# Time mixing begun in eight of the iterations 2 to 12 instead of iterations 5 to 12, its results kept in DRAM, and every helper step, plain product and low part placed by kind of iteration

## The chip, the cores and the metric

One core of a Trainium2 chip runs the whole program. The metric is the device time of one launch in microseconds (us). The kernel before took 924.7 us, the median of 3 runs (924.21 to 929.85). The profiled execution is one further run: 924.3 us, of which its trace spans 922.5 us.

## The reference

The input x is 8 sequences of 512 tokens with 128 channels, all fp32. Four residual layers follow each other, each on a layer norm of x:

```python
x = x + attention(norm(x))          # one head, causal, 128 channels
x = x + ffn(norm(x))                # 32 experts of width 64, top 4, capacity, and a shared expert
x = x + attn_b(norm(x))             # RWKV: time mixing, then channel mixing
x = x + ffn(norm(x))                # the same ffn and weights again
```

Inside attn_b, time mixing is a layer norm (ln1), three mixes of a token with the one before it, three 128x128 products for k, v and r, a recurrence over the 512 tokens with running maximum (wkv), a gate sigmoid(r), and an output product. Its result `u2 = u + time mixing` then goes into channel mixing: a layer norm (ln2), mixes, a 128x512 product, relu and square, a 512x128 product and a gate. The expert ffn is computed densely: `silu(x w1) * (x w3) * routing weight`, times w2, for all 32 experts in pairs.

## The kernel before

**Iterations and slots.** The ffn is the backbone. It runs for 8 sequences in layer 0 and for 8 in layer 1, so there are 16 iterations g = 0 to 15. An iteration has 17 units: 16 pairs of experts (`PAIRS`) and the shared expert. Each of the engines' programs walks `slot` from 0 to 16 (17 on VectorE, ScalarE and GpSimd), does unit `slot`, and between the units does steps of the other layers, each at a slot that is written out by hand. Nothing plans this at run time. Each engine works through its own list in order, so a step that waits holds up all units behind it on that engine.

**A unit.** TensorE multiplies the 512 tokens by w1 and w3 into PSUM banks `pa` and `pb`, two of each (L742 to L744). Operands are split into a high and a low part, so one product is three matmuls. ScalarE applies silu, or tanh in the slots of `TANH_UNITS` (L526, L528). VectorE multiplies with `pb` into `m_v` (L1043; with tanh L1049 and L1055). GpSimd multiplies with the routing weight `m_wb` into `m_h` (L418). Then the down product. On a split unit ScalarE copies the high part `m_hh` (L667), VectorE or GpSimd subtracts it to get the low part `m_hl` (L309), and TensorE does three matmuls (L760 to L762). On a native unit TensorE takes `m_h` itself in one plain fp32 product (L754, two records in the trace). `NATIVE` and `NATIVE_UNITS` say which: units 1, 3, ..., 15 of iterations 5 to 12, none elsewhere. `LOW_ON_POOL` says which low parts GpSimd makes.

TensorE may write the pair of banks of unit p only when VectorE has done `m_v` of unit p - 2, and VectorE may write `m_v` of unit p only when GpSimd has done `m_h` of unit p - 2.

**What shares the iterations.** `att` is attention of a sequence, `pro` is norm and router of the next iteration's sequence, `tmix` is time mixing and `cmix` is channel mixing:

| iteration | steps beside the ffn |
|---|---|
| 0 to 4 | att (sequence g + 2), pro |
| 5 | att, pro, tmix 0 |
| 6 to 12 | pro, tmix g - 5, cmix g - 6 |
| 13 | pro, cmix 7 |
| 14 | pro |
| 15 | none |

`cmix` begins with the output product of time mixing (TensorE L907) and the sum into `t_u2` (VectorE L1277), and it reads `t_u2` in SBUF until slot 10.

**VectorE in time mixing.** In slots 0 to 9: row statistics, the three mixes (L1213), the maximum scan (L1218) and the exponents (L1223 to L1228). In slots 11 to 17: two scans (L1233, L1235), products and sums (L1239 to L1247), four reciprocals (L1304), and the last two products (L1259, L1264).

**Queues.** SyncE issues all DMAs but two. `spread_weights(q)` waits for the router's result `r_wT` (ScalarE L581), writes it to DRAM (L345), waits for that, and reads it back with broadcast in four groups of four units, two 512 KB transfers each (L365), into a ring of two groups. Group 2 waits until GpSimd has done unit 3 of the iteration. Outputs are stored from the same queue (L371).

Of the kernel before, what the change touches and what calls it, by code (L numbers as in the profile page):

```python
# [9 lines left out]

# [47 lines left out]
N_MATS = 12  # L58


def hybrid_kernel(nc, x_in, att_mats, mats, key_in, vecs, w_gate, w1_in, w3_in, w2_in, x_out):
    with ExitStack() as ctx:  # L62
# [9 lines left out]
        def wide(ap):  # L72
# [114 lines left out]

        w_scratch = nc.dram_tensor("w_scratch", [2 * B, GROUPS, GP, 2, S], F32, kind="Internal").ap()
# [8 lines left out]
            "m_hl_dve m_hl_pool m_y m_ys m_yT m_x in_w2f "  # L197
# [47 lines left out]
        def native(g, p):  # L245

            return g in NATIVE and p in NATIVE_UNITS

# [17 lines left out]
        def front(step):  # L266

            step(att=1, pro=0, lead=5)
# [9 lines left out]
        def low_on_pool(g, p):  # L278

            return p in LOW_ON_POOL[sum(g >= first for first in POOL_FROM) - 1]  # L280

# [34 lines left out]
        def out_bank(tmix, cmix):  # L316

            return pq if tmix is None and cmix is None else pv
# [7 lines left out]
        def _(sp):  # L326
# [14 lines left out]

            def spread_weights(q):
# [4 lines left out]
                for j in range(GROUPS):  # L347
# [37 lines left out]
        def _(pool):  # L385
# [42 lines left out]
            def pro_step(q, slot):  # L428
                if slot == 2:
                    rsqrt(r_rs[:, :], r_ve[:, :], "r_vedone", q + 1, "r_rstd")  # L430
                if slot == 6:
# [5 lines left out]
            def time_step(m, slot):  # L437
                if slot == 0:
                    rsqrt(t_rs[:, :], t_ve[:, :], "t_ve", 2 * m + 2, "t_rstd")
                if slot == 4:  # L440
# [3 lines left out]
                if slot == 8:  # L444
# [4 lines left out]
                if slot == 9:  # L449
# [5 lines left out]
            def channel_step(m, slot):  # L455
                if slot == 10:
                    pool.wait_ge(sig["t_u2"], m + 1)
                    pool.wait_ge(sig["t_u"], m + 1)
# [4 lines left out]
                if slot == 6:  # L463
# [3 lines left out]
            def iteration(g=None, att=None, tmix=None, cmix=None, pro=None, lead=0):  # L467
                for slot in range(-lead, UNITS + 1):
# [5 lines left out]
                    if att is not None and slot == 0:  # L474
                        rsqrt(a_rs[:, :], a_ve[:, :], "a_vedone", att + 1, "a_rstd")
                    if cmix is not None:
# [905 lines left out]
```

## Time and profile before

| | |
|---|---|
| median of 3 runs | 924.7 us |
| profiled execution, span of its trace | 924.3 us, 922.5 us |
| start until unit 0 of iteration 0 | 62.4 us |
| TensorE (PE) busy | 818.3 us, 89% |
| VectorE (DVE) busy | 741.4 us, 80% |
| GpSimd (POOL) busy | 633.9 us, 69% |
| ScalarE (ACT) busy | 537.9 us, 58% |
| DMA, mean busy share of 16 engines by slice | 0 to 9 tenths, mostly 3 or 4 |

The busy time of TensorE is modelled: consecutive matmuls overlap in it, so what a matmul costs is read from the start of one to the start of the next. The boundary of an iteration is here the start of its first matmul into `pa`. Those starts lie at 62.4, 110.5, 159.4, 208.3, 260.0, 308.9, 371.9, 431.1, 489.9, 548.8, 607.6, 666.4, 725.3, 784.2, 835.4 and 875.7 us.

### The profile page before, as it was taken

Reading aid. Unit: us, or ns where it says so; the run is one execution under the profiler, and the core shown is the slowest. Engines: PE = TensorE matmul, PEld = TensorE weight load, DVE = VectorE, ACT = ScalarE, POOL = GpSimd, SP = SyncE. Lnnn points to the kernel's source line nnn. Section 1 sums busy time; section 2 is a strip of 40 time slices with the busy share of each in tenths; the row PEclk is TensorE's granted clock in tenths of the full one; section 3 lists DMA queues with packets and bytes.
Section 4 is the critical chain, followed back from the end, with each engine's and each line's share of the span. In section 5 each row is a group of like instructions: output and inputs, shape, how many; then the busy total and the mean of one; then the engine's idle time right before and its main releaser. Section 6 shows DMA issues by size and latency. Waiting matters only on the chain. (4 is left out here: it accounts for less than half of the span.)

```text
span 922.5 us, 12867 instructions
## 1 busy us (share of the span) xinstructions
PE 818.3 (89%) x3874; PEld 627.0 (68%) x3874; DVE 741.4 (80%) x1593; ACT 537.9 (58%) x1002; POOL 633.9 (69%) x467
## 2 busy tenths in 40 slices
PE   4579999998999986988979899898898998999997
PEld 2357777777777764766757667586675766778785
DVE  3557767686777779899898998998989989787764
ACT  2246566664656664673855747557476574575654
POOL 5417777777687865685767858678587686576675
PEclk9599999999999999999999999899999999999999
DMA  9033333425243430614305242143332441425262
GB/s 305 0 95 77 82 78 82 102 53 131 49 96 91 95 92 3 137 47 94 74 21 128 56 89 55 43 108 90 66 75 57 95 103 43 99 60 135 74 141 66
DMA packets 46500, 78.12 MB, mean 85 GB/s; under 512 B 3168, under 2 KB 12512, under 8 KB 46048
## 3 DMA queue, kind: packets, MB, share of 16 engines
q1 hardware_dynamic: 46144, 77.10, 35.6%
q8 instruction: 32, 0.52, 0.3%
q10 hardware_dynamic: 288, 0.20, 0.1%
q14 instruction: 36, 0.29, 0.1%
HBM read 74.14 MB, written 3.15 MB: 84 GB/s over the span
## 5 line engine op out<-in xcount | busy, mean ns | idle before, releaser
L418 POOL TENSOR_TENSOR m_h<-m_v,m_wb 128x512 f32<-128x512 f32 x256 | 366.2, 1436 | 207.3 <-DVE m_v L1043 106.5
L526 ACT ACTIVATE m_th<-pa 128x512 f32<-128x512 f32 x232 | 138.3, 596 | 198.9 <-PE pa L744 168.2
L309 DVE TENSOR_TENSOR m_hl<-m_h,m_hh 128x512 fp32r<-128x512 f32 x130 | 111.4, 858 | 81.3 <-ACT m_hh L667 81.2
L742 PE MATMUL pa<-m_xh,w1h 128*128 128x512 f32 x272 | 143.3, 527 | 31.4 <-DVE m_v L1055 31.0
L1043 DVE TENSOR_TENSOR m_v<-m_th,pb 128x512 f32<-128x512 f32 x216 | 145.9, 676 | 16.4 <-ACT m_th L526 9.4
L667 ACT ACTIVATE m_hh<-m_h 128x512 fp32r<-128x512 f32 x208 | 130.6, 628 | 35.8 <-POOL m_h L418 34.8
L742 PE MATMUL pb<-m_xh,w3h 128*128 128x512 f32 x272 | 110.2, 405 | 10.1 <-DVE m_v L1043 9.8
L309 POOL TENSOR_TENSOR m_hl<-m_h,m_hh 128x512 fp32r<-128x512 f32 x78 | 108.0, 1384 | 7.1 <-ACT m_hh L667 7.1
L744 PE MATMUL pb<-m_xh,w3l 128*128 128x512 f32 x272 | 108.6, 399 | 0.0
L744 PE MATMUL pa<-m_xh,w1l 128*128 128x512 f32 x272 | 108.3, 398 | 0.0
L743 PE MATMUL pa<-m_xl,w1h 128*128 128x512 f32 x272 | 108.1, 397 | 0.0
L743 PE MATMUL pb<-m_xl,w3h 128*128 128x512 f32 x272 | 108.1, 397 | 0.0
L742 PEld LDWEIGHTS pa<-m_xh,w1h 128*128 128x128 f32 x272 | 52.3, 192 | 58.2 <-DVE m_v L1055 40.7
L760 PE MATMUL py<-m_hh,w2h 128*128 128x512 f32 x208 | 83.2, 400 | 2.6 <-POOL m_hl L309 2.6
L762 PE MATMUL py<-m_hl,w2h 128*128 128x512 f32 x208 | 82.9, 399 | 0.0
L761 PE MATMUL py<-m_hh,w2l 128*128 128x512 f32 x208 | 82.6, 397 | 0.0
L742 PEld LDWEIGHTS pb<-m_xh,w3h 128*128 128x128 f32 x272 | 51.7, 190 | 28.1 <-DVE m_v L1043 16.1
L754 PE MATMUL py<-m_h,w2f 128*128 128x512 f32 x128 | 65.2, 591 | 0.0
L743 PEld LDWEIGHTS pa<-m_xl,w1h 128*128 128x128 f32 x272 | 52.5, 193 | 17.7 <-issue 13.9
L744 PEld LDWEIGHTS pb<-m_xh,w3l 128*128 128x128 f32 x272 | 52.2, 192 | 12.1
L744 PEld LDWEIGHTS pa<-m_xh,w1l 128*128 128x128 f32 x272 | 51.9, 191 | 12.0
L743 PEld LDWEIGHTS pb<-m_xl,w3h 128*128 128x128 f32 x272 | 52.0, 191 | 11.5
(211 smaller groups left out, 1651.2 us busy)
## 6 DMA issues: line engine op xcount, KB each, us to landing
m_wb<-w_scratch SPq DMA_DIRECT2D x126, 512.0 KB, 6.5
x_sb<-in_x SPq DMA_DIRECT2D x8, 256.0 KB, 7.2
m_wb<-in_w SPq DMA_DIRECT2D x2, 1024.0 KB, 6.9
x_out<-x_sb SPq DMA_DIRECT2D x8, 256.0 KB, 6.9
f_kk<-in_w SPq DMA_DIRECT2D x1, 1024.0 KB, 9.9
w_scratch<-r_wT SPq DMA_DIRECT2D x16, 64.0 KB, 1.6
m_wb<-w_scratch SPq DMA_DIRECT2D x8, 128.0 KB, 3.0
mt<-in_mats SPq DMA_DIRECT2D x1, 768.0 KB, 8.1
```

What stands on the lines that cost most here:

```text
L309: eng.tensor_tensor(m_hl[:, at, :], hidden(g, p), m_hh[:, at, :].bitcast(F32), ALU.subtract)\
L418: pool.tensor_tensor(hidden(g, p), gated(g, p), m_wb[:, p % (GRING * GP), :], ALU.mult).then_inc(sig["m_h"], 1)
L526: ins = act.activation(m_th[:, p % 2, :], pa[p % 2][:, :], ACT.Silu)
L667: act.activation(m_hh[:, halves_at(g, p), :], hidden(g, p), ACT.Copy).then_inc(sig["m_hh"], 1)
L742: pe.matmul(ps[:, :], high[:, p, :], xh, start=True, stop=False)
L743: pe.matmul(ps[:, :], high[:, p, :], xl, start=False, stop=False)
L744: return pe.matmul(ps[:, :], low[:, p, :], xh, start=False, stop=True)
L754: pe.matmul(py[:, :], w2f[:, NATIVE_UNITS.index(p), :], hidden(g, p), start=False, stop=False)\
L760: pe.matmul(py[:, :], w2h[:, p, :], hh, start=(p == 0), stop=False)
L761: pe.matmul(py[:, :], w2l[:, p, :], hh, start=False, stop=False)
L762: pe.matmul(py[:, :], w2h[:, p, :], hl, start=False, stop=(p == UNITS - 1)).then_inc(sig["m_y"], 1)
L1043: dve.tensor_tensor(gated(g, p), m_th[:, r, :], pb[r][:, :], ALU.mult).then_inc(sig["m_v"], 1)
```

## The change

The results of the time mixing of sequences 0 to 5 (`KEPT`) are written to a DRAM tensor `u_scratch` and read back into `t_u2` in the iteration of their channel mixing. Time mixing is cut into `begin` (up to the exponentials and the r product), `finish` (from the two scans to the gate) and `out` (output product and sum). `begin` is done in iterations 2, 3, 4, 5, 6, 8, 10, 12, `finish` in 2, 3, 4, 5, 7, 9, 11, 12, and `out` in the iteration after `finish`. Attention and channel mixing stay in their iterations. Each iteration has one of seven modes, and each step's slot is a tuple over modes:

| iteration | mode | beside ffn and pro |
|---|---|---|
| 0, 1 | 0 | att |
| 2 to 5 | 1 | att, begin, finish, and out from 3 on |
| 6, 8, 10 | 3 | cmix, begin, out |
| 7, 9, 11 | 4 | cmix, finish |
| 12 | 2 | cmix, begin, finish, out |
| 13 | 5 | cmix, out |
| 14, 15 | 6 | none |

```diff
-NATIVE = range(B - 3, 2 * B - 3)
 NATIVE_UNITS = (1, 3, 5, 7, 9, 11, 13, 15)
-LOW_ON_POOL = ((0, 4, 6, 7, 8, 9, 11, 12, 14, 15), (0, 4, 8, 12), (6, 14), (6, 9, 12, 15), (2, 9, 14))
-POOL_FROM = (0, B - 3, B - 2, 2 * B - 3, 2 * B - 2)
+MODES = (0, 0, 1, 1, 1, 1, 3, 4, 3, 4, 3, 4, 2, 5, 6, 6)
+NATIVE = ((9,), (1, 3, 5, 7, 9, 11, 13, 15), (1, 3, 5, 7, 9, 11, 13, 15), (1, 3, 5, 7, 9, 13, 15), (1, 3, 5, 7, 9, 11, 13, 15), (1,), (9, 13))
+LOW_ON_POOL = ((4, 6, 7, 8, 11, 12, 14, 15), (4, 6, 8, 12, 14), (6, 10, 14), (6, 11, 14), (0, 6, 8, 12, 14), (0, 6, 9, 12, 15), (2, 4, 8, 14))
+KEPT = 6
+BEGIN_AT = {2: 0, 3: 1, 4: 2, 5: 3, 6: 4, 8: 5, 10: 6, 12: 7}
+BEGINS = {1: 0, 2: 1, 3: 2}
+FINISHES = {1: 0, 2: 1, 4: 2}
+OUTS = {1: 0, 2: 1, 3: 2, 5: 3}
...
+def plan(g):
+    finishes = {2: 0, 3: 1, 4: 2, 5: 3, 7: 4, 9: 5, 11: 6, 12: 7}
+    outs = {3: 0, 4: 1, 5: 2, 6: 3, 8: 4, 10: 5, 12: 6, 13: 7}
+    return Plan(g, g + 2 if g < LATE else None, BEGIN_AT.get(g), finishes.get(g), outs.get(g),
+                g - LATE if LATE <= g < LATE + B else None, g + 1 if g < 2 * B - 1 else None, MODES[g])
...
+        def kept(eng, m):
+            if m < KEPT:
+                eng.wait_ge(sig["u_in"], 16 * m + 16)
+            else:
+                eng.wait_ge(sig["t_u2"], m + 1)
...
+            def keep(it):
+                if it.cmix is not None and it.cmix < KEPT:
+                    sp.wait_ge(sig["u_out"], 16 * it.cmix + 16)
+                    if it.cmix > 0:
+                        sp.wait_ge(sig["f_x"], 2 * it.cmix)
+                    sp.dma_start(wide(t_u2[:, :, :]), u_scratch[it.cmix]).then_inc(sig["u_in"], 16)
+                if it.out is not None and it.out < KEPT:
+                    sp.wait_ge(sig["t_u2"], it.out + 1)
+                    sp.dma_start(u_scratch[it.out], wide(t_u[:, :, :])).then_inc(sig["u_out"], 16)
...
                         sp.wait_ge(sig["m_h"], done(PAIRS * (q - 1) + GP * (GROUPS - GRING + j + 1)))
+                    if j == GRING:
+                        keep(plan(q))
```

Some of the slots on VectorE, TensorE and ScalarE (tuples of two are over modes 0 and 1; tuples of three are over the modes of `BEGINS` or `FINISHES` in the order of their values; tuples of four are over modes 2 to 5):

```diff
             # VectorE
-                if slot == 1:
+                if slot == (2, 0)[mode]:            # attention: normalise a_xn
-                if slot == 9:
+                if slot == (9, 8, 9)[mode]:         # begin: maximum scan, exponents
-                if slot == 11:
+                if slot == (13, 13, 12)[mode]:      # finish: two scans, two products
-                if slot == 12:
+                if slot == (13, 14, 12)[mode]:      # finish: two sums
-                if slot == 14:
+                if slot == (13, 16, 13)[mode]:      # finish: reciprocal 0
-                if slot == 15:
+                if slot == (16, 17, 15)[mode]:      # finish: reciprocal 1
-                if slot == 14:
+                if slot == (15, 16, 14)[mode]:      # finish: reciprocals 2, 3
-                if slot == 3:
-                    dve.wait_ge(sig["t_u2"], m + 1)
+                if slot == (3, 5, 5, 2)[mode]:      # channel mixing: row statistics of t_u2
+                    kept(dve, m)
...
             # TensorE
-                if slot == 3:
+                if slot == (4, 2)[mode]:            # attention: transposes of a_xn
-                if slot == 10:
+                if slot == (10, 9, 12, 12)[mode]:   # channel mixing: first key product
...
             # ScalarE
-                if slot == 14:
+                if slot == (14, 13, 14, 15, 15, 17, 14)[mode]:   # router: r_wT
```

(The comments are this document's, the rest is the diff.) The instructions themselves are the same ones, except for the 12 transfers of 256 KB and the exchange of split for plain products.

## Rows read from the trace of the kernel before

**Rows 1.** Busy time by iteration: 2 (first row), 4, 5, 9, 10, 13

```profile
core 0: us, PE busy (x) PEld busy (x) DVE busy (x) ACT busy (x) POOL busy (x), PEclk, DMA share, GB/s
...
159.40:208.30 48.90, 46.61 (x239) 37.45 (x238) 36.09 (x90) 30.59 (x59) 37.53 (x30) 1.00 0.38 87
...
260.00:308.90 48.90, 46.60 (x240) 37.44 (x239) 35.92 (x90) 30.59 (x59) 37.57 (x30) 1.00 0.39 88
308.90:371.90 63.00, 53.31 (x244) 38.90 (x243) 53.08 (x115) 34.09 (x66) 41.72 (x32) 0.97 0.31 70
...
548.80:607.60 58.80, 54.29 (x249) 40.76 (x249) 54.14 (x107) 36.31 (x66) 42.07 (x29) 0.94 0.32 74
607.60:666.40 58.80, 52.03 (x249) 38.58 (x248) 54.14 (x107) 36.48 (x66) 42.09 (x29) 1.00 0.34 77
...
784.20:835.40 51.20, 48.16 (x245) 37.93 (x245) 38.58 (x82) 32.39 (x59) 32.30 (x24) 1.00 0.38 88
```

**Rows 2.** The same: early in iteration 5; iterations 9 and 13 cut at unit 11

```profile
311.00:330.00 19.00, 18.62 (x90) 14.20 (x88) 15.83 (x47) 13.08 (x29) 17.45 (x14) 1.00 0.55 122
...
548.80:579.40 30.60, 30.50 (x138) 22.61 (x137) 26.31 (x61) 21.81 (x44) 22.57 (x16) 1.00 0.43 98
579.40:607.60 28.20, 23.79 (x114) 18.15 (x113) 27.82 (x47) 14.50 (x23) 19.50 (x13) 0.88 0.20 47
784.20:813.50 29.30, 27.61 (x130) 21.48 (x130) 22.54 (x47) 18.45 (x35) 18.74 (x14) 1.00 0.42 90
813.50:835.40 21.90, 20.55 (x116) 16.45 (x115) 16.04 (x36) 13.93 (x24) 13.55 (x11) 1.00 0.34 85
```

**Rows 3.** Timeline of TensorE, iteration 9: start, duration, instruction, idle time before it

```profile
577.52 0.39 PE L760 MATMUL py<-m_hh,w2h 128*128 128x512 f32 x1
...
578.21 0.39 PE L942 MATMUL pv<-f_xh,key_h 128*128 128x512 f32 x1
...
581.14 1.02 PE L754 MATMUL py<-m_h,w2f 128*128 128x512 f32 x2
582.00 1.05 PE L921 MATMUL pu<-mt,a_pT 128*128 128x128 f32 x8
...
586.88 0.79 PE L742 MATMUL pa<-m_xh,w1h 128*128 128x512 f32 x1 [3.12 <-DVE m_v L1055]
```

**Rows 4.** Timeline of VectorE, iteration 9, the end of time mixing

```profile
590.52 1.21 DVE L1233 TENSOR_TENSOR_SCAN t_aa<-t_ea,t_xk 128x512 f32<-128x512 f32 x1
...
594.99 0.68 DVE L309 TENSOR_TENSOR m_hl<-m_h,m_hh 128x512 fp32r<-128x512 f32 x1
...
596.19 0.68 DVE L1244 TENSOR_TENSOR t_xr<-t_xr,t_eb 128x512 f32<-128x512 f32 x1
596.79 1.79 DVE L1247 TENSOR_TENSOR t_n<-t_n,t_xv 128x512 f32<-128x512 f32 x1
...
600.92 2.57 DVE L1304 RECIPROCAL t_ri<-t_xr 128x128 f32<-128x128 f32 x3
...
603.95 0.94 DVE L1304 RECIPROCAL t_ri<-t_xr 128x128 f32<-128x128 f32 x1
...
605.35 0.68 DVE L1259 TENSOR_TENSOR t_ri<-t_n,t_ri 128x512 f32<-128x512 f32 x1
606.07 1.65 DVE L1264 SCALAR_TENSOR_TENSOR t_n<-t_r,t_ri 128x512 f32<-128x512 f32 x1
```

**Rows 5.** Waits in iterations 0 to 4: total us, times, longest

```profile
PE pu L720 <- DVE a_xn L1019: 10.4, 5, 2.9
...
DVE a_xn L1019 <- POOL a_rs L403: 7.9, 5, 2.7
```

**Rows 6.** Timeline of iteration 9: GpSimd at unit 3, then VectorE at unit 5

```profile
559.92 1.29 POOL L418 TENSOR_TENSOR m_h<-m_v,m_wb 128x512 f32<-128x512 f32 x1 [0.19 <-DVE m_v L1043]
...
564.08 0.68 DVE L1043 TENSOR_TENSOR m_v<-m_th,pb 128x512 f32<-128x512 f32 x1
```

**Rows 7.** The output stores of 256 KB (L371), from issue to landing

```profile
DMA to landing us min/median/max: 2.3/6.9/7.2
```

More of the change, by code:

```diff
@@ L9 @@
 from contextlib import ExitStack
+from typing import NamedTuple
 import concourse.bass as bass
@@ L58, with begun @@
 N_MATS = 12
+class Plan(NamedTuple):
+    g: int | None = None
+    att: int | None = None
+    begin: int | None = None
+    finish: int | None = None
+    out: int | None = None
+    cmix: int | None = None
+    pro: int | None = None
+    mode: int = 0
+def begun(g):
+    return sum(1 for at in BEGIN_AT if at < g)
+def plan(g):
[3 more added lines that the diff above has]
+                g - LATE if LATE <= g < LATE + B else None, g + 1 if g < 2 * B - 1 else None, MODES[g])
 def hybrid_kernel(nc, x_in, att_mats, mats, key_in, vecs, w_gate, w1_in, w3_in, w2_in, x_out):
@@ L266, in front @@
         def front(step):
-            step(att=1, pro=0, lead=5)
+            step(Plan(att=1, pro=0), lead=5)
         def is_late(g):
@@ L278, in low_on_pool @@
         def low_on_pool(g, p):
-            return p in LOW_ON_POOL[sum(g >= first for first in POOL_FROM) - 1]
+            return p in LOW_ON_POOL[MODES[g]]
         pool_lows = [k for k in split_units if low_on_pool(*divmod(k, UNITS))]
@@ L674, in out_copy, with iteration @@
                 act.activation(m_y[:, :], py[:, :], ACT.Copy).then_inc(sig["m_ys"], 1)
-            def iteration(g=None, att=None, tmix=None, cmix=None, pro=None, late=False, lead=0):
+            def iteration(it, lead=0):
+                g = it.g
                 for slot in range(-lead, UNITS + 1):
                     if g is not None and slot < UNITS:
-                        unit(g, slot, late)
+                        unit(g, slot, is_late(g))
                         split_high(*unit_before(g, slot, SPLIT_LAG))
-                    if slot == 3:
+                    if slot == (2, 2, 3, 3, 3, 3, 3)[it.mode]:
@@ L695, in _ @@
-            for g in range(1, B - 3):
-                iteration(g, att=g + 2, pro=g + 1)
-            iteration(B - 3, att=B - 1, tmix=0, pro=B - 2)
-            iteration(B - 2, tmix=1, cmix=0, pro=B - 1, late=True)
-            iteration(B - 1, tmix=2, cmix=1, pro=B, late=True)
-            iteration(B, tmix=3, cmix=2, pro=B + 1, late=True)
-            for g in range(B + 1, 2 * B - 3):
-                iteration(g, tmix=g - (B - 3), cmix=g - (B - 2), pro=g + 1, late=True)
-            iteration(2 * B - 3, cmix=B - 1, pro=2 * B - 2, late=True)
@@ L704, in _ @@
-            iteration(2 * B - 2, pro=2 * B - 1, late=True)
-            iteration(2 * B - 1, late=True)
+                    if it.att is not None:
+                        att_step(it.att, slot, it.mode)
+                    if it.cmix is not None:
+                        channel_step(it.cmix, slot, it.mode - 2)
+                    if it.pro is not None:
+                        pro_step(it.pro, slot + lead, it.cmix, it.mode)
+                    if it.begin is not None:
+                        time_begin(it.begin, slot, it.pro, BEGINS[it.mode])
@@ L706, in _ @@
+            iteration(Plan(att=0))
+            front(iteration)
+            for g in range(2 * B):
+                iteration(plan(g))
             for p in range(UNITS - SPLIT_LAG, UNITS):
@@ L889, in time_step @@
                     turn(pq, t_hn, "t_tr")
-                if slot == 8:
+                if slot == (9, 8, 8)[mode]:
                     pe.wait_ge(sig["t_xk"], 3 * m + 3)
```

363 lines of the change are left out of this document (170 added, 193 removed).

## The prediction

> **What bounds the kernel now.** I read the busy time of the engines by iteration first, since the change moves work between iterations and removes none. An iteration with attention alone takes 48.9 us with VectorE busy 36; one with time and channel mixing takes 58.8 us with VectorE busy 54.1; iteration 5, with attention and time mixing, takes 63.0 us with VectorE busy 53.1; iteration 13, with channel mixing alone, takes 51.2 us with VectorE busy 38.6 [rows 1]. So there are light and heavy iterations for VectorE, and TensorE has 47 to 54 us in all of them.
>
> Cutting iterations 9 and 13 at unit 11 shows which engine sets the pace where. In the first 30.6 us of iteration 9 TensorE is busy 30.5 and VectorE idles 4.3. In the remaining 28.2 us VectorE is busy 27.8 and TensorE 23.8. The same last six units of iteration 13, which have no time mixing, take 21.9 us [rows 2]. So a heavy iteration is bound by TensorE in its first eleven units and by VectorE in its last six. The timeline shows how: TensorE stands 3.1 us before unit 12 until VectorE has given up a bank [rows 3]. What fills VectorE there is the second half of time mixing: 590.52 to 594.99 (4.5 us), 596.19 to about 598.5 (2.3), 2.6 and 0.9 of reciprocals, and 2.4 from 605.35 to its end, together 12.7 us [rows 4]. The change takes this half out of iterations 6, 8 and 10 and the other half out of 7, 9 and 11; the price is that iterations 2, 3 and 4 become heavy.
>
> **Iterations 2 to 5.** They take 212.5 us now (159.4 to 371.9). Each becomes like iteration 5. VectorE then has 53.1 us [rows 1], less one low part (0.7, as at 594.99), plus, in 3 to 5, the sum into `t_u` (0.7 as well, an operation of that size) and the last two products of the time mixing before, 2.4 [rows 4], which for iteration 5 now fall after its end. That makes 52.4 for iteration 2 and 55.5 for each of 3, 4 and 5. To this comes what VectorE idles. Iteration 5 idles 9.9 now, iteration 9 idles 4.7 [rows 1]. The least that rows support is 3.2 in the early stretch of iteration 5 plus 0.4 in the late stretch of iteration 9, 3.6 [rows 2]. Iteration 5 is the only one of its kind now and shares its slots with iterations 0 to 4 and 6 to 12; with slots of its own, and the low parts spread otherwise, I take 4.1, between that least and the 4.7 of iteration 9. The sum is 56.5 + 3 x 59.6 = 235.3, so +22.8 us. The ends: 3.6 gives +20.8, and 9.9 gives +46.
>
> TensorE's addition there, three plain products and eight native units a piece, is covered: a native unit costs 0.86 us (581.14 to 582.00) against 0.69 for a split one (577.52 to 578.21) [rows 3], so eight cost 1.4 us, under a VectorE that has 55. If VectorE were no longer the bound, these 1.4 us would appear four times.
>
> **Iterations 6 to 11.** They take 353.4 us now (371.9 to 725.3). In 6, 8 and 10 the second half of time mixing is gone. Their first eleven units stay at 30.6, as TensorE's work there is the same; their last six fall to the 21.9 of iteration 13, since VectorE has 27.8 - 12.7 = 15.1 us left there. Two native units in that stretch add 0.3. That is 52.8, and I take 53.0. In 7, 9 and 11 the first half is gone and the second stays. First part: 29.3 as in iteration 13, plus five native units (0.9), minus the output product of time mixing (about 0.4, an estimate: half of the 0.9 that four times as many columns of plain fp32 take in one native product), 29.8. Last part: VectorE's 16.0 of iteration 13 plus 12.7, minus three low parts that are now native or on GpSimd (2.1), minus the last two products, which fall into the next iteration's part bound by TensorE (2.4): 24.2, which is over TensorE's 21.9 and so counts. That is 54.0. Together 3 x 53.0 + 3 x 54.0 = 321.0, so -32.4 us. The ends: -20 if the burst of 12.7 us in four or five slots is not absorbed by two banks and TensorE pays another 2 us in each of the six, and -40 if the last parts of all six come down to 21.9.
>
> **The reload.** `t_u2` is read back in iterations 6 to 11. SyncE issues it after GpSimd's unit 3, which ends at 561.2 in iteration 9; VectorE comes to the statistics after its unit 5, at 564.8 [rows 6]. That leaves 3.6 us. No transfer out of this scratch is in the trace. A 256 KB transfer took 2.3 us at the least and 6.9 in the median, where others lie ahead of it [rows 7]. At that point the ring's transfers of group 1, issued at the iteration's start, are through, and those of group 2 are issued behind the reload. So I take 2.3 and a cost of nothing, hidden by units 4 and 5; the other end is 0.2 + 6.9 - 3.6 = 3.5 us per iteration, 21 us. The six stores stand in the same queue in front of group 2, which GpSimd wants four units later, over 8 us; they cost nothing unless the queue is late by more than that. SyncE's own waits before both are for things done an iteration, or two slots, earlier; behind them only group 2 and 3 and the next router's write are queued.
>
> **The small rest.** In iterations 0 to 4 VectorE waits up to 2.7 us for GpSimd's `a_rs`, which stands behind unit 0, and TensorE then stands 2.9 us for the normalised attention input [rows 5]. In iterations 0 and 1 both steps come one slot later, which I count as 0.5 each, -1.0 us. It could be nothing, or 2 each. In iterations 2 to 5 the step moves to slot 0, which makes VectorE wait there for GpSimd; that lies in the idle time I counted. Iterations 12 to 15 and the start keep their work but for a low part here and a native unit there, and slots: -0.5, between -3 and +3, as nothing in the trace prices a slot by itself.
>
> **Sum.** -1.0 + 22.8 - 32.4 + 0 - 0.5 = -11.1 us against the profiled execution's 924.3, that is 913.2. The median of the runs shown is 0.4 higher than that execution, which is less than I can claim to know: I put it at 913.
>
> **A rule on the clock.** The granted clock of TensorE is 0.88 in the last part of iteration 9, where it waits for VectorE, and 1.00 in that of iteration 13 [rows 2]. Yet iteration 9 with a mean of 0.94 and iteration 10 with 1.00 both take 58.8 us [rows 1]: the lower of the two levels, 1.2 instead of 2.4 GHz, falls into time that VectorE sets. So the sum has no term for it. The Trainium skill ("TensorE: Matmul & The Clock Gate", "Part 1: The HAM clock gate") says that an idle array is put to 1.2 GHz and is given 2.4 GHz again once busy, and warns of kernels whose waits bring this on again and again; by that rule the change would pay in iterations 2 to 4 and be paid in 6 to 11. As a mechanism of this kernel it is the fourth rival below.
>
> **The rivals.** About 1% (9 us) is what a measurement of this kernel can tell from no change.
> - *Iterations 2 to 5 pack no better than iteration 5 does today.* With VectorE idle 7.0 in each, halfway between the 4.1 that I took and the 9.9 of today, they sum to 218.9 + 28.0 = 246.9, 11.6 more: 925. For it speaks that attention and time mixing want `pq`, `pu` and VectorE in the same late slots, and that in the new slots two scans, two products, two sums and a reciprocal all stand in slot 13, about 7.7 us at once. Against it, that in iteration 9 bursts like this cost VectorE nothing, only TensorE. 0.20.
> - *The reload is late (slower).* Its place is VectorE in slot 5 of iterations 6 to 11, and behind it GpSimd's statistics root, ScalarE's normalise and the key products, which in iterations 6, 8, 10 come at slot 9 instead of 10 while the statistics come two slots later. At 6.9 us to landing the price is 21 us: 934. It makes the kernel slower once more than 1.9 us per iteration are lost, that is, with a landing after 5.3 us or a chain to the key products that is short by as much; beyond 3.4 us it is slower by over 1%. 0.14.
> - *VectorE ceases to bind anywhere for long.* Iterations 2 to 5 at the idle of 3.6 (-2), the last parts of 6 to 11 all at 21.9 (-7.5): 903. 0.15.
> - *The clock follows the waits and counts.* Iteration 5 has 0.97 where iterations 2 and 4 have 1.00 [rows 1]: 3% of 60 us in three iterations, +5; iterations 6 to 11 from about 0.97 to 1.00, 3% of 53 in six, -10: 908. 0.05, as iterations 9 and 10 speak against it.
>
> **How the numbers follow.** The forecast itself gets 0.46, with a range of its own of 905 to 921. About seven tenths of it lie below 915.5, where faster by over 1% begins, so faster is 0.32 + 0.15 + 0.05 = 0.52. The rest of it and nearly all of the first rival is within 1%: 0.14 + 0.18 = 0.32. Slower is the second rival and the tail of the first, 0.16. The range that leaves out about two in ten, half of the reload's case and the ends of the others, is 894 to 932.
>
> **What would show it.** In the trace after: iterations 2 to 5 at 56 to 60 us with VectorE idle under 5 in each; iterations 6 to 11 at 52 to 55, with the last six units of 6, 8, 10 near 22 us and no more than 25 in 7, 9, 11; no wait of VectorE for the reload of over 0.5 us; landing of the reload at 2.3 to 3.5 us. The forecast is wrong in its first term if iterations 2 to 5 are over 62 us, in its second if 6 to 11 sum to over 333, and in the third if VectorE's statistics of `t_u2` wait for a transfer.

## The result, and the profile after

The kernel after takes 901.8 us, the median of 4 runs (900.4 to 905.0), against 926.6 us of the kernel before on the same chip: a ratio of 0.9735, 95% interval 0.9691 to 0.9779. Forecast were 913 us with a range of 894 to 932. The direction held and the time is in the range, 11 us under the forecast. The profiled execution has a span of 903.2 us against the 922.5 us of before. Sums by iteration, here and below, come from one profiled execution of each kernel; medians come from all of its runs.

The first view is again the busy time by iteration: 0, 3 and 5 (first three rows), the two parts of 6 cut at unit 11, the two parts of 7, then 8, 9, 12 and 13. They answer to [rows 1, 2].

```profile
core 0: us, PE busy (x) PEld busy (x) DVE busy (x) ACT busy (x) POOL busy (x), PEclk, DMA share, GB/s
62.50:106.90 44.40, 43.63 (x223) 34.33 (x222) 34.95 (x89) 28.98 (x56) 31.40 (x25) 1.00 0.32 82
215.30:273.90 58.60, 53.41 (x248) 37.85 (x247) 51.05 (x120) 33.24 (x65) 39.07 (x31) 1.00 0.32 79
332.40:392.40 60.00, 55.16 (x248) 38.52 (x247) 50.42 (x120) 33.23 (x65) 38.38 (x30) 0.97 0.30 75
392.40:430.00 37.60, 34.33 (x148) 24.86 (x147) 30.43 (x71) 24.17 (x47) 26.91 (x21) 0.95 0.51 117
430.00:449.00 19.00, 19.00 (x105) 14.89 (x103) 11.01 (x30) 13.18 (x22) 13.90 (x12) 1.00 0.08 24
449.00:476.60 27.60, 26.29 (x118) 19.60 (x117) 19.11 (x42) 16.76 (x32) 20.91 (x17) 1.00 0.59 132
476.60:497.50 20.90, 20.90 (x116) 16.73 (x115) 20.39 (x43) 12.75 (x21) 14.89 (x11) 1.00 0.12 26
497.50:553.90 56.40, 52.99 (x252) 40.21 (x250) 41.63 (x95) 36.67 (x67) 38.72 (x31) 0.97 0.38 92
553.90:602.50 48.60, 47.26 (x233) 36.34 (x231) 39.79 (x83) 29.55 (x52) 35.61 (x27) 1.00 0.42 96
709.40:768.10 58.70, 53.79 (x250) 39.51 (x249) 50.84 (x102) 36.08 (x66) 43.93 (x32) 0.97 0.35 80
768.10:815.80 47.70, 47.55 (x246) 38.41 (x244) 37.99 (x84) 32.14 (x58) 35.39 (x26) 1.00 0.37 84
```

The last parts of iterations 6 to 11 are now TensorE from end to end (19.00 of 19.0, 20.90 of 20.9). What is left idle lies in the first part of 6, 8 and 10 and in the heavy iterations 2 to 5 and 12. The boundaries are the first matmuls into `pa`, at 62.5, 106.9, 153.7, 215.3, 273.9, 332.4, 392.4, 449.0, 497.5, 553.9, 602.5, 660.0, 709.4, 768.1, 815.8, 856.9 and 903.2 us. In sums:

| iterations | before | after | difference | forecast |
|---|---|---|---|---|
| 0, 1 | 97.0 | 91.2 | -5.8 | -1.0 |
| 2 to 5 | 212.5 | 238.7 | +26.2 | +22.8 |
| 6, 8, 10 | 176.9 | 170.5 | -6.4 | -17.9 |
| 7, 9, 11 | 176.5 | 146.5 | -30.0 | -14.5 |
| 12 to 15 | 197.3 | 193.8 | -3.5 | -0.5, start included |
| all, with the start | 922.5 | 903.2 | -19.3 | -11.1 |

TensorE's waits before and after are the second view (total us, times, longest). First the kernel before:

```profile
engine line waited for: us in total, times, longest us
PE pa L742 <- DVE m_v L1055: 31.0, 17, 3.1
PE pu L720 <- DVE a_xn L1019: 15.1, 7, 3.9
...
PE pb L742 <- DVE m_v L1043: 9.8, 10, 2.1
PE pq L880 <- DVE r_carry L1193: 9.5, 8, 1.4
```

And the kernel after. The wait before `pa` (31.0 us) is gone, the one for `r_carry` is 1.4 us, and those for `a_xn` and before `pb` are 7.3 and 6.5. The two waits for ScalarE at the head are in attention and in the norms:

```profile
engine line waited for: us in total, times, longest us
PE pu L869 <- ACT a_p L600: 10.9, 3, 6.2
PE pu L758 <- ACT a_xn L698: 8.0, 7, 2.2
PE pq L908 <- ACT t_r L652: 7.9, 4, 2.0
PE pu L758 <- DVE a_xn L1053: 7.3, 5, 3.8
PE pb L780 <- DVE m_v L1077: 6.5, 9, 1.5
```

In sum, TensorE is idle 74.6 us of the 860.1 between its first matmul into `pa` and the end before, and 50.5 of 840.7 after, and its busy time is 4.7 us longer. So the gain in the profile is waits of TensorE that are gone.

The reload is the third view: its issues, who waited, and its landing. It answers to [rows 7].

```profile
L388 SPq DMA_DIRECT2D t_u<-u_scratch x6: 325/326/337, 406.1 to 673.5; - x6
...
  DVE a_st L1035: 4.4, 6
...
DMA to landing us min/median/max: 2.1/2.9/3.4
```

Its landing of 2.9 us is what was forecast (2.3 to 3.5), but VectorE waits for it in every one of the six iterations. The timelines of GpSimd, VectorE and TensorE in iteration 8 (497.5 to 553.9) show why, and answer to [rows 6]:

```profile
509.85 1.29 POOL L471 TENSOR_TENSOR m_h<-m_v,m_wb 128x512 f32<-128x512 f32 x1
```

```profile
511.61 1.27 DVE L1077 TENSOR_TENSOR m_v<-m_th,pb 128x512 f32<-128x512 f32 x2
514.15 0.88 DVE L1035 BATCH_NORM_STATS2 a_st<-t_u 128x6 f32<-128x128 f32 x4 [1.27 <-DMA t_u<-u_scratch]
...
516.87 0.16 DVE L1047 SCALAR_TENSOR_TENSOR a_nm<-a_mv,a_rs 128x4 f32<-128x4 f32 x1 [1.12 <-POOL a_rs L456]
```

```profile
519.26 0.66 PE L758 MATMUL pu<-ident,a_xn 128*128 128x128 f32 x4 [2.15 <-ACT a_xn L698]
...
523.61 0.63 PE L898 MATMUL pv<-wg,t_v 128*128 128x32 f32 x4 [1.18 <-ACT m_xh L617]
```

GpSimd's unit 3 ends at 511.14, and VectorE is through with unit 5 at 512.88. The slack is 1.7 us, not the 3.6 read in iteration 9 of before, and with some 3 us of landing VectorE idles 1.27. Behind it stand GpSimd's root, ScalarE's normalise and TensorE, which has then nothing to do for 2.15 us.

### The profile page after: what moved, and what is told of

Same layout as the page of the kernel before. It is cut to its first block and busy times, and to the rows that moved or that the text cites. A ratio compares the mean times of both kernels' runs of the same rounds, so it can differ in the third digit from the quotient of the medians.

```text
span 903.2 us, 12742 instructions
## 1 busy us (share of the span) xinstructions
PE 822.2 (91%) x3846; PEld 617.6 (68%) x3846; DVE 684.3 (76%) x1567; ACT 522.6 (58%) x974; POOL 609.4 (67%) x465
## 5 line engine op out<-in xcount | busy, mean ns | idle before, releaser
L471 POOL TENSOR_TENSOR m_h<-m_v,m_wb 128x512 f32<-128x512 f32 x256 | 350.0, 1378 | 173.9 <-DVE m_v L1077 79.7
L714 ACT ACTIVATE m_hh<-m_h 128x512 fp32r<-128x512 f32 x180 | 113.0, 628 | 42.5 <-POOL m_h L471 41.3
L342 POOL TENSOR_TENSOR m_hl<-m_h,m_hh 128x512 fp32r<-128x512 f32 x76 | 103.4, 1361 | 44.4 <-ACT m_hh L714 44.4
L342 DVE TENSOR_TENSOR m_hl<-m_h,m_hh 128x512 fp32r<-128x512 f32 x104 | 85.3, 821 | 53.3 <-ACT m_hh L714 52.7
L792 PE MATMUL py<-m_h,w2f 128*128 128x512 f32 x184 | 96.4, 606 | 0.0
L798 PE MATMUL py<-m_hh,w2h 128*128 128x512 f32 x180 | 71.5, 397 | 2.4 <-POOL m_hl L342 2.4
L800 PE MATMUL py<-m_hl,w2h 128*128 128x512 f32 x180 | 71.3, 396 | 0.0
L799 PE MATMUL py<-m_hh,w2l 128*128 128x512 f32 x180 | 70.8, 393 | 0.0
L780 PEld LDWEIGHTS pa<-m_xh,w1h 128*128 128x128 f32 x272 | 51.7, 190 | 21.1 <-issue 15.3
L782 PEld LDWEIGHTS pa<-m_xh,w1l 128*128 128x128 f32 x272 | 51.7, 190 | 11.8
```

The costliest lines, as they stand in the source:

```text
L342: eng.tensor_tensor(m_hl[:, at, :], hidden(g, p), m_hh[:, at, :].bitcast(F32), ALU.subtract)\
L471: pool.tensor_tensor(hidden(g, p), gated(g, p), m_wb[:, p % (GRING * GP), :], ALU.mult).then_inc(sig["m_h"], 1)
L714: act.activation(m_hh[:, halves_at(g, p), :], hidden(g, p), ACT.Copy).then_inc(sig["m_hh"], 1)
L780: pe.matmul(ps[:, :], high[:, p, :], xh, start=True, stop=False)
L782: return pe.matmul(ps[:, :], low[:, p, :], xh, start=False, stop=True)
L792: pe.matmul(py[:, :], w2f[:, NATIVE_UNITS.index(p), :], hidden(g, p), start=False, stop=False)\
```

## The experiments

Twelve kernels were run. Each time stands as a ratio to the kernel before on the same chip; 0.974 is the kernel after. The profiled execution is not always typical of its kernel: with the early reload it took 887.3 us where the median is 898.2, and with the old placement 922.0 where the median is 928.4. Part of both differences lies ahead of the first matmul into `pa`, which comes at 57.9 and 57.3 us instead of 62.2 in the second profile of the kernel after.

**The result again.** The kernel after itself, without an edit.

> The changed kernel once more, to stand beside the next three on one chip. Theory and rival both expect 901 to 905 us, 0.971 to 0.978 of the kernel before, and the same sums by iteration: about 239 us for iterations 2 to 5, 171 for 6, 8 and 10, 147 for 7, 9 and 11.

902.35 us (901.4 to 903.5), 0.974 [0.9717, 0.9763]. This is the time that the edits of the kernel after are held against. The two kernels that move the reload alone and the one with the old slot of `a_xn` ran on the same chip as it, the others on two other chips.

### How the gain divides: two times two

**The old plan with all the rest of the change.** Time mixing in iterations 5 to 12, nothing kept in DRAM.

```diff
-MODES = (0, 0, 1, 1, 1, 1, 3, 4, 3, 4, 3, 4, 2, 5, 6, 6)
+MODES = (0, 0, 0, 0, 0, 1, 2, 2, 2, 2, 2, 2, 2, 5, 6, 6)
-KEPT = 6
+KEPT = 0
...
+    finishes = BEGIN_AT
+    outs = {g + 1: m for g, m in BEGIN_AT.items()}
```

> The changed kernel with the plan of the kernel before: time mixing begins and finishes in iterations 5 to 12, nothing is kept in DRAM, channel mixing 0 follows in iteration 6. Slots, native units and low parts are those of the new modes (0 in iterations 0 to 4, 1 in 5, 2 in 6 to 12, 5 in 13, 6 in 14 and 15). Theory, from the changed kernel's trace: iterations 0 to 4 at 46 to 47 (232), 5 at 59, 6 to 12 at 58.5 (410), the rest 135, with the start 62.5: 899. So the spread itself would be worth nothing or cost a little, and the new slots and placement of low parts bring all of the 24 us. Rival, the prediction's own reason: the spread brings at least 9 us, so this takes 911 or more.

909.81 us, 0.981 [0.9778, 0.9842]. This is near the rival (911 or more) and 11 us over the theory, whose sum by iteration was too low for 6 to 11. Iterations 2 to 5 sum to 201.6, 6 to 11 to 359.7 (58.4 to 61.0 each).

**The new plan with the old placement** of plain products and low parts, by number of iteration instead of kind.

```diff
-            return p in NATIVE[MODES[g]]
+            return 5 <= g < 13 and p in NATIVE_UNITS
...
-            return p in LOW_ON_POOL[MODES[g]]
+            old = ((0, 4, 6, 7, 8, 9, 11, 12, 14, 15), (0, 4, 8, 12), (6, 14), (6, 9, 12, 15), (2, 9, 14))
+            return p in old[sum(g >= first for first in (0, 5, 6, 13, 14)) - 1]
```

> The changed kernel with the native units and the low parts of the kernel before, by iteration (units 1, 3, ..., 15 native in iterations 5 to 12 alone; ten low parts on GpSimd in 0 to 4). Theory: iterations 2 to 4, heavy now, get 17 low parts each with ten on GpSimd, so GpSimd and ScalarE get 8 steps more in each: 4 us more in each of the three, and 7, 9, 11 with two instead of five low parts on GpSimd 1 us each: 15 us more than the changed kernel. Rival: placement is worth little because TensorE binds: under 4 us more.

928.42 us, 1.0027 [0.9988, 1.0065]: the whole gain is gone, 26 us and not the 15 of the theory. Iterations 2 to 5 take 258.0 us instead of 238.7; this is 3:

```profile
214.51:282.68 68.17, 54.58 (x257) 40.08 (x255) 61.37 (x124) 37.90 (x74) 48.89 (x37) 0.97 0.30 73
```

VectorE is busy 61.4 us there, 10.3 more than in the same iteration of the kernel after, and GpSimd 48.9 against 39.1.

**Only the plain products placed as before**, the low parts as after.

```diff
-            return p in NATIVE[MODES[g]]
+            return 5 <= g < 13 and p in NATIVE_UNITS
```

> The kernel after, with the plain down products alone placed as before (units 1, 3, ..., 15 of iterations 5 to 12, none in 0 to 4 and 13 to 15); the low parts that GpSimd makes stay placed by kind. It splits the 26 us that both placements together were worth. In iterations 2 to 4 this puts back eight split units each, so eight copies on ScalarE and some five low parts of 0.7 us on VectorE. Theory (VectorE is the bound in 2 to 5, and the plain products are what makes room there): 2 to 4 take 3.5 to 5 us more each, 6 to 11 change by under 3 in sum, and the time is 912 to 920 us. Rival (the low parts on GpSimd are what counts, since GpSimd is late for m_h in the heavy iterations): 2 to 4 take at most 1.5 us more each and the time is 902 to 907 us.

921.04 us, 0.9951 [0.9919, 0.9983]. Iterations 2 to 4 take 3.9, 6.0 and 5.6 us more than after, 6 to 11 take 1.7 less. The theory holds, its size was a little low (912 to 920). This is iteration 3:

```profile
220.79:285.47 64.68, 55.53 (x256) 41.43 (x255) 58.13 (x128) 37.35 (x73) 40.54 (x31) 0.95 0.31 71
```

Of the 26 us of both placements the plain products bear 19 and the low parts 7.

**Old plan and old placement, new slots.** Both edits together.

> The kernel before in its plan (time mixing in iterations 5 to 12, nothing kept in DRAM) and in its plain products and low parts, with only the slots of the steps as in the kernel after. It prices the slots alone. Before is 925.4; the new slots with the new placement and the old plan took 909.8. Theory (most of those 15.6 us are the slots of attention's and time mixing's steps, which take away the waits for a_xn and spread the burst at slot 11): 910 to 915 us, with iterations 0 to 4 shorter by 1.5 to 3.5 us each and 6 to 12 at 58 to 61. Rival (the placement gives them, as it gave 26 us under the new plan): 919 to 925 us, with iterations 0 to 4 shorter by under 1 us.

922.46 us, 0.9968 [0.993, 1.0006]. In time the rival holds: the slots alone are worth about 3 us, and the interval includes none. By iteration it doesn't, since iterations 0 and 2 to 4 are shorter by 1.5 to 4.2 us and the gain is lost again behind them. Iterations 2 to 4 are 47.4 against 48.9 to 51.7 before, but 6 to 11 are 60 to 61 against 59. The four medians:

| new slots, and | old plan | new plan |
|---|---|---|
| old placement | 922.5 | 928.4 |
| new placement | 909.8 | 902.3 |

So spreading time mixing costs 6 us without the placement (the intervals of 922.5 and 928.4 overlap a little) and gives 7.5 with it. In this order, the 23.1 us from 925.4 to 902.3 are 2.9 of slots, 12.7 of placement and 7.5 of spreading. Slots and placement go by mode, and modes 3 and 4 exist in the new plan alone, so the two columns don't differ in the plan and in nothing else. Neither of the last two does alone what it does with the other.

### The reload

**The reload ahead of the wait for GpSimd's unit 3** and so early in the iteration; its store stays where it was.

```diff
+                    if j == GRING:
+                        fetch(plan(q))
                     if j >= GRING:
                         sp.wait_ge(sig["m_h"], done(PAIRS * q + GP * (j - GRING + 1)))
```

> SyncE issues the reload of t_u2 before it waits for GpSimd's unit 3, so right behind the transfers of group 1, some 8 us earlier. Theory: in iterations 6, 8 and 10 VectorE waits 1.3 us for the reload and TensorE later stands 2.2 us for the input of the ln2 transposes that comes out of the same chain; with the wait gone, TensorE gets about 1 us back in each of the three, and nothing in 7, 9 and 11 where the chain has slack: 3 us less, 0.997 of the changed kernel. Rival: the chain is held by ScalarE's and GpSimd's other steps (t_u waits for the store, the root for unit 5), the wait of VectorE only moves to the root: no difference within 1 us.

898.20 us (887.3 to 902.1), 0.9664 [0.9621, 0.9708]. No engine waits for the reload, although its landing is longer now (2.0, 4.6 and 8.8 us at the least, in the median and at the most). The median is 4.2 us under that of the kernel after, of which this is the better version; the theory had 3. TensorE's waits in iterations 6 to 11 fall from 14.2 us in the profile of the kernel after to 10.7, which fits. Iterations 6, 8 and 10 sum to 163.9 instead of 171.0, but this is the profile of the fastest run, and not all of the 7.1 us is the reload's: the granted clock in the first eleven units of iterations 8 and 10 is 1.00 here and 0.96 and 0.91 in the second profile of the kernel after. By these clocks some 5 us of the 7.1 are the clock's (an estimate: 4% of 38.0 and 9% of 38.9).

**The reload behind the transfers of group 2.**

```diff
                     for h in range(2):
                         sp.dma_start(m_wb[H * h:H * (h + 1), at:at + GP, :],
                                      w_scratch[q, j, :, h, :].partition_broadcast(H)).then_inc(wb_in[j], 16)
+                    if j == GRING:
+                        fetch(plan(q))
```

> SyncE issues the reload of t_u2 behind the two 512 KB transfers of group 2 and so lands it some 5 us later (6.5 to 8 us after GpSimd's unit 3 instead of 3). This prices the rival of the prediction. Theory that it was a near miss: VectorE waits 4 to 5 us more in slot 5 of all six iterations, of which TensorE's two banks absorb about 2: 6 x 3 = 18 us more than the changed kernel, about 921. Rival, that the early part has slack for it: under 6 us more, as the late parts of 7, 9 and 11 are light.

953.81 us, 1.0297 [1.026, 1.0334], 51 us more than the kernel after, where the theory had 18. VectorE's statistics wait 39.1 us in six iterations. This is iteration 8 of it (517.2 to 582.6): SyncE's issues, VectorE's wait, and two stretches of the iteration.

```profile
530.92 1.26 SPq L420 DMA_DIRECT2D m_wb<-w_scratch  x2
532.28 0.55 SPq L388 DMA_DIRECT2D t_u<-u_scratch  x1
```

```profile
540.13 0.87 DVE L1039 BATCH_NORM_STATS2 a_st<-t_u 128x6 f32<-128x128 f32 x4 [7.87 <-DMA t_u<-u_scratch]
```

```profile
533.60:546.30 12.70, 3.61 (x18) 2.58 (x17) 4.87 (x15) 4.51 (x11) 3.95 (x4) 0.77 0.36 88
546.30:582.61 36.31, 35.14 (x163) 26.95 (x161) 23.26 (x46) 22.45 (x37) 23.78 (x19) 0.89 0.17 42
```

Iterations 6 to 11 sum to 365.6 us, 56.6 more than with the early reload (309.0), for 39.1 us of waits: 1.4 us of time for 1 us of wait. Against the second profile of the kernel after (317.5, with 5.3 us of waits) it is 48.1 for 33.8, 1.4 as well. The second stretch shows a part of the difference: TensorE is busy 35.1 of 36.3 us, but at a granted clock of 0.89. The same stretch in iteration 8 of the early kernel takes 32.6 us at 1.00.

**The reload earlier still, and the whole chain from it two slots earlier.**

```diff
+                    if j == 1:
+                        fetch(plan(q))
...
-                if slot == (3, 5, 5, 2)[mode]:      # VectorE: statistics; GpSimd: their root
+                if slot == (3, 3, 3, 2)[mode]:
-                if slot == (5, 5, 5, 3)[mode]:      # VectorE: shifts
+                if slot == (5, 4, 4, 3)[mode]:
-                if slot == (6, 7, 6, 5)[mode]:      # ScalarE: normalise
+                if slot == (6, 5, 5, 5)[mode]:
-                if slot == (7, 7, 7, 6)[mode]:      # TensorE: its transposes
+                if slot == (7, 6, 6, 6)[mode]:
```

> The kernel after, with the reload of t_u2 issued ahead of group 1's transfers (early in the iteration) and, in iterations 6 to 11, the chain from it two slots earlier: row statistics on VectorE and their root on GpSimd in slot 3 instead of 5, the shifts in 4, normalise in 5, TensorE's first step in 6. Theory (iterations 6, 8 and 10 are long because TensorE stands for the chain reload, statistics, root, normalise, keys, and a chain that starts earlier takes those waits away): the three sum to 153 to 160 us against 170.5 after and 163.9 with the earlier reload alone, their first eleven units near 33 instead of 37.6; 7, 9 and 11 stay at 144 to 148; the time is 884 to 894 us. Rival (the earlier reload already gave what there was, and the rest of 6, 8 and 10 is work of VectorE and GpSimd at those units, which only changes its place): the three stay at 162 to 167 and the time is 896 to 900 us, or more if the chain now stands before the mask and router steps of slots 3 to 5.

913.65 us, 0.9862 [0.9822, 0.9902]: a miss of both theory and rival. Iterations 6, 8 and 10 sum to 179.0, 15 more than with the early reload alone. The chain is ready two slots earlier only in the list: TensorE still stands 1.58 us before its transposes, now one unit earlier, and ScalarE stands 3.2 us before the normalise, and VectorE 3.7 us for a high part that ScalarE makes behind it. What they had still to do then falls together. VectorE's mixes of iteration 8, first here, then in the kernel with the early reload:

```profile
522.54 1.18 DVE L1251 SCALAR_TENSOR_TENSOR t_xk<-t_n,vec,t_h 128x512 f32<-128x512 f32 x1
523.65 1.52 DVE L1251 SCALAR_TENSOR_TENSOR t_xv<-t_n,vec,t_h 128x512 f32<-128x512 f32 x1
525.09 1.75 DVE L1251 SCALAR_TENSOR_TENSOR t_xr<-t_n,vec,t_h 128x512 f32<-128x512 f32 x1
526.76 1.75 DVE L1332 SCALAR_TENSOR_TENSOR a_p<-a_g,vec,a_xT 128x512 f32<-128x512 f32 x1
528.44 1.76 DVE L1332 SCALAR_TENSOR_TENSOR a_pT<-a_g,vec,a_xT 128x512 f32<-128x512 f32 x1
```

```profile
509.73 0.96 DVE L1251 SCALAR_TENSOR_TENSOR t_xk<-t_n,vec,t_h 128x512 f32<-128x512 f32 x1
510.61 0.74 DVE L1251 SCALAR_TENSOR_TENSOR t_xv<-t_n,vec,t_h 128x512 f32<-128x512 f32 x1
511.27 0.74 DVE L1251 SCALAR_TENSOR_TENSOR t_xr<-t_n,vec,t_h 128x512 f32<-128x512 f32 x1
512.94 0.75 DVE L1332 SCALAR_TENSOR_TENSOR a_p<-a_g,vec,a_xT 128x512 f32<-128x512 f32 x1 [0.93 <-POOL a_g L521]
513.61 0.75 DVE L1332 SCALAR_TENSOR_TENSOR a_pT<-a_g,vec,a_xT 128x512 f32<-128x512 f32 x1
```

The same five operations take 8.0 us instead of 3.9. In the first kernel GpSimd works without a gap beside them, from 520.9 to 529.6. TensorE's waits in iterations 6 to 11 grow from 10.7 to 18.9 us, mostly those for `x_sb` (1.9 to 6.2) and `t_xr` (none to 2.9); the rest of the 15 us goes with the clock (1.00 in iteration 8 of the early reload, 0.94 here).

### The slot of the attention norm

**`a_xn` back to its old slot in iterations 0 and 1.**

```diff
-                if slot == (2, 0)[mode]:            # VectorE: a_xn
+                if slot == (1, 0)[mode]:
-                if slot == (4, 2)[mode]:            # TensorE: its transposes
+                if slot == (3, 2)[mode]:
```

> In iterations 0 and 1 (and the first two attentions) VectorE normalises a_xn in slot 1 and TensorE transposes it in slot 3, as before, instead of 2 and 4. Iterations 0 and 1 took 97.0 us before and 91.2 after, where I had expected 96. Theory: this one slot is most of it, since VectorE waited for GpSimd's a_rs with unit 2 behind it: 4 us more than the changed kernel. Rival: the lighter GpSimd (three low parts fewer beside one native unit) and the other slots did it: under 1 us more.

906.88 us, 0.9791 [0.9761, 0.9822], 4.5 more than the kernel after. Iterations 0 and 1 sum to 94.4 in its profile, 2.2 more than in the second profile of the kernel after (92.2) and 3.2 more than in the first (91.2).

### What binds the last part of a heavy iteration

**The kernel before with reciprocals of one column** instead of 128. It leaves out most of the division of time mixing.

```diff
-                part = slice(P * i, P * (i + 1))
+                part = slice(P * i, P * i + 1)
```

> The kernel before with the same shortened reciprocals (most of the division left out). If VectorE sets the late part of each of its eight iterations with time mixing, as the prediction had it, this saves nearly the whole 3.3 us in each, 24 us or a ratio of 0.974. Rival, that TensorE or the chains through ScalarE take over at once: under 12 us.

927.69 us, 1.0009 [0.9972, 1.0047]: the rival holds. VectorE's busy time in iteration 9 falls from 54.1 to 51.4 us and the iteration stays as it was (58.8):

```profile
545.27:604.14 58.87, 52.10 (x251) 38.62 (x249) 51.44 (x106) 36.41 (x66) 41.56 (x29) 1.00 0.31 71
```

**The kernel before with scans and first products of one column.** It leaves out most of the recurrence.

```diff
-                    dve.tensor_tensor_scan(out=t_aa[:, 1:1 + S], data0=t_ea[:, 0, :], data1=t_ev[:, :], initial=0.0,
+                    dve.tensor_tensor_scan(out=t_aa[:, 1:2], data0=t_ea[:, 0, 0:1], data1=t_ev[:, 0:1], initial=0.0,
```

(So for `t_bb`, `t_n1` and `t_d1` too.)

> The kernel before, with the two scans and the two products behind them in time mixing made on one column instead of 512 (this leaves out most of the recurrence). It takes 1.2 + 1.2 + 0.7 + 0.7 = 3.8 us from VectorE in slots 11 and 12 of iterations 5 to 12, just ahead of the place where TensorE stands 3.1 us for unit 12's bank. Theory (the late part of a heavy iteration is bound by this burst of VectorE at slots 11 and 12, not by its work in slots 13 to 17): TensorE's 3.1 us are gone and nothing takes their place: iterations 6 to 12 take 55 to 56.5 us instead of 58.8, and the time is 903 to 910 us. Rival (the bound is the sum of VectorE's work over the last six units, as the prediction had it, or some other chain): the shortened reciprocals gave nothing, and this gives nothing either, or only its share: iterations 6 to 12 at 58 to 59 us, time 918 to 926 us.

904.05 us (902.8 to 909.1), 0.9771 [0.9722, 0.982]. As much of VectorE's time is gone as with the reciprocals: its busy time in iteration 9 falls to 51.4 us again, by 2.7 and not by the 3.8 that was expected. (The scan into `t_bb` took 2.24 us before, not 1.2, and other operations became longer.) Here it counts: iterations 6 to 12 sum to 394.3 us instead of 412.3. But not as the theory had it. These are TensorE's waits for VectorE with the short reciprocals:

```profile
PE pa L742 <- DVE m_v L1055: 31.3, 17, 3.1
...
PE pb L742 <- DVE m_v L1043: 10.2, 12, 2.1
PE pq L880 <- DVE r_carry L1193: 9.6, 8, 1.4
```

and with the short scans:

```profile
PE pa L742 <- DVE m_v L1055: 28.1, 16, 3.1
...
PE pq L880 <- DVE r_carry L1193: 2.9, 4, 0.9
...
PE pb L742 <- DVE m_v L1043: 2.4, 5, 0.9
```

The 3.1 us before unit 12 stay. That bank is given up behind the exponents of `begin` and the router's softmax, ahead of the scans. Mostly gone are the two waits behind the scans, before the router's transposes (L880) and before the `pb` of unit 14. So VectorE holds TensorE up in a heavy iteration at three points: one behind the exponents of slots 10 and 11, two behind the scans of slots 11 and 12, and none behind the reciprocals.

**The kernel after with the short reciprocals.**

> The changed kernel with each of the four reciprocals of time mixing on 1 column instead of 128 (this leaves out most of the division, so the output of attn_b is not the reference's). VectorE loses about 3.3 us per time mixing. Theory: in 7, 9 and 11 VectorE no longer binds, so nothing is gained there; in iterations 2 to 5 and 12 it binds in part: 5 x 2 = 10 us less than the changed kernel. Rival: VectorE's burst still sets the late part everywhere: 8 x 3 = 24 us less.

894.98 us, 0.9648 [0.9611, 0.9684], 7.4 less than the kernel after. Iterations 7, 9 and 11, where the reciprocals stand, sum to 148.1, against 146.4, so they win nothing there. What the profile shows lies in 2 to 5 (237.1 to 235.6) and in 6, 8 and 10 (171.0 to 164.6), which have none but in the iteration ahead of them. No wait there is much shorter: VectorE waits for the reload as long as ever (4.7 us). What differs is the granted clock in the first eleven units of 8 and 10, 1.00 here against 0.96 and 0.91, the same as in the profile with the early reload. TensorE's busy time in these two stretches is 64.6 us instead of 69.8, which is 5.2 of the 6.4 us. Why the clock stayed up was not settled.

## Why the prediction was right or wrong

**What bounds the kernel** was half right. TensorE sets the first part of an iteration, and VectorE holds up the last one. But "bound by VectorE" was read from 27.8 busy of 28.2 us [rows 2], and the sums then took every microsecond of VectorE there at its full price. The two kernels with short operations refute this: VectorE is busy 51.4 us instead of 54.1 in iteration 9 of both, and with the short reciprocals this is worth nothing, with the short scans 2.6 us in each of iterations 6 to 12 (18.0 in seven). VectorE held TensorE up at two or three points, and it was busy between them because there was work for it.

**Iterations 2 to 5** were forecast at 235.3 us and take 238.7. They lie at 58.4 to 61.6 us against the 56 to 60 that were named. The size is nearly right, its make-up is not: VectorE is busy 47.1, 51.1, 50.9 and 50.5 us, not 52.4 to 55.5, and idle 7.5 to 14.5, not 4.1. TensorE, priced as covered, is busy 53.4 to 55.2. The first rival's condition, VectorE idle 7.0 or more, came true without its price, since VectorE's own sum was too high.

**Iterations 6 to 11** were forecast at 321.0 and take 317.0. Here two errors cancel. In 7, 9 and 11 the last part is 20.9 us where 24.2 were forecast. The step that failed is "24.2, which is over TensorE's 21.9 and so counts": VectorE is busy 20.4 there and TensorE 20.9. In 6, 8 and 10 the step that failed is "their first eleven units stay at 30.6". They take 37.6 in iteration 6: 3.8 of the difference is TensorE's busy time (34.3 against 30.5). About 2 of that is work that the new slots put ahead of unit 11 and that is missing in the last part (19.0 instead of the forecast 22.2): with the early reload, where the clock in the first parts of 8 and 10 is 1.00, TensorE is busy 32.3 and 32.6 there. The other 1.8 is the same work at a granted clock of 0.95. The rest, 3.2 us, is waits; iteration 8 has 2.15 for `a_xn`, at the end of the chain from the reload, and 1.18 for `m_xh` of the router. That makes -30.0 and -6.4 us where -14.5 and -17.9 were forecast. A small term of the first part of 7, 9 and 11 was mis-sized too: the output product of time mixing takes 0.80 us in iteration 9 of before (557.45 to 558.25), not about 0.4.

**The reload** was costed at nothing. Landing was right. What failed was the slack of 3.6 us, taken from an iteration of a kind that the change does away with. In iteration 9 of before GpSimd's unit 3 ended 12.4 us after the start and VectorE was free at 16.0 [rows 6]; in iteration 8 of after the two are at 13.6 and 15.4, and 1.7 us are left. Its cost, by the kernel with the early reload, is 4.2 us in the whole, not 0 and far from the 21 of the slower rival. That rival was near all the same. With two transfers of 512 KB in front, the landing is 7.8 us at the most, and the kernel is slower than before by 3%, at 954 us. The rival's 934 had 3.5 us of wait in each iteration where 6.5 were measured, and nothing for the clock behind the waits.

**The small rest** is the term that made the forecast too high: -9.3 us measured (-5.8 and -3.5) against -1.5. The other terms miss by +3.4 and -4.0 and nearly cancel. In iterations 0 and 1 the later slot of `a_xn` is worth 2.2 to 3.2 us in the profile and 4.5 in the median, not 1.0; within the "or 2 each" of the text. The placement is worth another 1.1 to 2.1 there (93.3 with the old one against 91.2 and 92.2). In 12 to 15 the old placement takes 197.3 us, as before, but the sum hides two things: iteration 13 keeps its gain with it (48.1 against 51.3 before), so that is the slots' or the moved steps', and iteration 15 takes 48.9 instead of 46.4, at a granted clock of 0.93. What the prediction left unpriced is the placement as such. It took it in with iteration 5 as its model, which has plain products, and so never asked what the plan would be worth without it: nothing at all, 928 us.

**The rivals.** Nearest in time is the third (903 us, VectorE ceases to bind). Of its terms the last parts of 6 to 11 at 21.9 held, and more (19.0 and 20.9); the one on iterations 2 to 5 did not. The fourth, the clock, did not make the bulk of the gain: TensorE's idle time accounts for it (74.6 to 50.5 us). A share of it can't be ruled out. The mean granted clock over all runs is 0.963 before and 0.973 after on one chip, and 0.965 with the old placement. One minus this clock is the most that the lower level can have cost, 34 us of 925.9 and 25 of 902.4, so at most 9 of the 24 us are the clock's (an estimate; no run holds the clock fixed). It decides on what a wait costs, as the late reload shows. Where TensorE was busy 3.6 of 12.7 us, the clock was 0.89 in the 36 us behind. The Trainium skill ("TensorE: Matmul & The Clock Gate", "HAM oscillation — how this bites in real kernels") describes just this, a wait for a transfer in each turn of a loop, each followed by work at half the clock; the trace agrees, with a clock of 0.77 in the stretch with the wait and 0.89 behind it. The price here is 1.4 us for each us that VectorE waits.

## What to carry to other kernels

An engine busy 98% of a stretch does not bind it everywhere: take the waits of the engine behind it, find the instruction ahead of each, and price only what stands before those. When work is moved so that stretches of a new kind arise, read no slack from the old ones, and issue a transfer as early as its buffer allows rather than just in time, since the place behind two transfers of 512 KB instead of ahead of them turned a gain of 2.6% into a loss of 3%. Spreading work over more stretches and making room in them are one change: each half alone was worth -6 and 13 us, both together 20.

## What was not expected of the hardware

VectorE's busy time fell from 741.4 to 684.3 us, though only 26 low parts left it (130 to 104, 26.1 us). Most of the rest is in operations that became shorter without any change to them. First before, then after:

```profile
L1019 DVE TENSOR_SCALAR a_xn<-x_sb,a_mv,a_rs 128x128 f32<-128x128 f32 x32 | 18.5, 639 | 10.2 <-POOL a_rs L403 10.2
...
L1178 DVE TENSOR_TENSOR r_ws<-r_sel,r_p 128x128 f32<-128x128 bf16 x16 | 13.6, 847 | 0.5
```

```profile
L1053 DVE TENSOR_SCALAR a_xn<-x_sb,a_mv,a_rs 128x128 f32<-128x128 f32 x32 | 11.7, 428 | 9.2 <-POOL a_rs L456 9.2
...
L1212 DVE TENSOR_TENSOR r_ws<-r_sel,r_p 128x128 f32<-128x128 bf16 x16 | 5.7, 354 | 0.6
```

The sum L1247 (L1283 after) is 1.79 us in iteration 9 of before, beside an `m_h` of GpSimd, and 0.68 in iteration 7 of after, where GpSimd stands from 485.4 to 489.7. Operations with one operand in PSUM, as `m_v`, and the reciprocals do not change (676 and 678 ns, 917 and 926). The Trainium skill ("GPSIMD Engine Reference", "8. Key points") says that GpSimd shares its SBUF interfaces with VectorE and gets in the way of VectorE's instructions in a 2-port mode or with two SBUF inputs; the trace agrees, with 0.68 against 1.79 us for one sum and 3.9 against 8.0 for the five mixes above. So what a slot costs on VectorE depends on what GpSimd has in the same one. Moving the chain by two slots made those five operations 4.1 us longer in iteration 8 without any work added. How much of the 5 us that iterations 6, 8 and 10 lost on average comes from this, and not from the waits and the clock, no run separates.
